# One block for the third attention, the second mixture's routing and its experts

## The reference, cut to what matters

```python
x = x + _L2_xattn_ref(_layernorm(x), ctx, ...)       # 8 heads of 64: softmax(q k / 8) v @ Wo + bo
x = x + _L2_ffn_ref(_layernorm(x), ...)

# _L2_ffn_ref, xf = the normalised tokens (N = 4096)
logits = xf @ Wr + br
topv, topi = top_k(logits, 2)
gates = softmax(topv)
sel = one_hot(topi, 8).sum(1)
rank = cumsum(sel, axis=0) - sel                     # place in the expert's queue, in token order
keep = (sel > 0) & (rank < 1024)                     # capacity
h = gelu(xg @ W1[e] + b1[e]);  out = h @ W2[e] + b2[e]   # xg: the kept tokens of expert e
final[token] += gate * out
```

## Time and profile before

| | us |
|---|---|
| median of three runs (1740.43 to 1750.24) | 1745.27 |
| the profiled execution | 1739.88 |
| its span in the profile | 1738.0 |
| TensorE busy in the span | 1367.1 (79%) |
| DVE busy | 1083.1 (62%) |
| ACT busy | 825.0 (47%) |
| POOL busy | 550.3 (32%) |

### The profile page before, as it was taken

The page is one execution under the profiler, slowest core; times in us unless marked ns, Lnnn a source line. Parts: engine busy times, 40 slices in busy tenths (PEclk is TensorE's granted clock), DMA queues, the critical chain, the costliest instruction groups (busy, mean ns, idle before and its releaser), DMA issues. The chain is left out here.

```text
span 1738.0 us, 43934 instructions
## 1 busy us (share of the span) xinstructions
PE 1367.1 (79%) x14972; PEld 1057.1 (61%) x14972; DVE 1083.1 (62%) x3255; ACT 825.0 (47%) x2117; POOL 550.3 (32%) x990
## 2 busy tenths in 40 slices
PE   6999979986499994149995999994148974678787
PEld 3677655553266674149995888874137763566566
DVE  4888738897899987424443766647401114789764
ACT  1666636665476672412221555541013335677565
POOL 4555411111211105730004644305730007842332
PEclk9999975788699995569997999995569995689798
DMA  4333200000000001137773211101136651111001
GB/s 145 132 112 110 110 27 2 3 3 3 17 23 21 23 17 38 50 112 205 206 205 91 55 40 43 29 12 39 47 110 194 195 150 46 38 24 35 1 13 37
DMA packets 111207, 120.11 MB, mean 69 GB/s; under 512 B 12736, under 2 KB 88512, under 8 KB 110912
## 3 DMA queue, kind: packets, MB, share of 16 engines
q1 hardware_dynamic: 83264, 91.67, 17.5%
q0 software_dynamic: 8192, 16.79, 3.4%
q10 hardware_dynamic: 19584, 9.44, 1.8%
HBM read 81.16 MB, written 36.70 MB: 68 GB/s over the span
## 5 line engine op out<-in xcount | busy, mean ns | idle before, releaser
L2234 PE MATMUL e_H<-e_xT,e_w_up 128*128 128x256 f32 x736 | 173.8, 384 | 0.0
L2080 DVE COPY e_xT<-e_pX 128x256 f32<-128x256 f32 x72 | 30.6, 425 | 216.0 <-PE e_pX L2223 216.0
L2234 PEld LDWEIGHTS e_H<-e_xT,e_w_up 128*128 128x128 f32 x736 | 136.5, 193 | 16.1
L2244 PE MATMUL e_pY<-e_w_down,e_h 128*128 128x128 f32 x992 | 124.4, 277 | 15.8 <-ACT e_h L2156 15.2
L2244 PEld LDWEIGHTS e_pY<-e_w_down,e_h 128*128 128x128 f32 x992 | 119.9, 192 | 27.0 <-issue 19.3
L2145 ACT ACTIVATE e_silu<-e_H 128x256 f32<-128x256 f32 x120 | 42.6, 382 | 162.8 <-DVE e_y L2100 89.7
L2276 POOL DMA_INDIRECT slots_in<-R,r_put x96 | 92.6, 964 | 39.9 <-issue 28.3
L2223 PE MATMUL e_pX<-W,e_rows 128*128 128x128 f32 x144 | 28.6, 282 | 95.1 <-DMA e_rows<-slots_in 93.8
L478 ACT ACTIVATE a_PT<-a_ST 128x1024 f32<-128x1024 f32 x64 | 65.6, 1025 | 77.5 <-PE a_ST L545 77.5
L433 DVE TENSOR_REDUCE a_mx<-a_S 128x8 f32<-128x1024 f32 x64 | 78.1, 1221 | 31.7 <-PE a_S L518 31.5
L2156 ACT ACTIVATE e_h<-e_H,e_w_down 128x256 f32<-128x256 f32 x128 | 50.2, 475 | 85.7 <-DMA e_w_down<-in_f_dram 49.6
(11 more groups left out here) (378 smaller groups left out, 3962.6 us busy)
## 6 DMA issues: line engine op xcount, KB each, us to landing
slots_in<-Y SPq DMA_DIRECT2D x32, 512.0 KB, 3.4
e_w_up<-in_f_dram SPq DMA_DIRECT2D x40, 384.0 KB, 3.1
e_w_down<-in_f_dram SPq DMA_DIRECT2D x32, 322.0 KB, 3.2
e_rows<-slots_in SPq DMA_DIRECT2D x72, 128.0 KB, 2.9
slots_out<-e_y ACTq DMA_DIRECT2D x72, 128.0 KB, 2.9
e_w_up<-in_f_dram SPq DMA_DIRECT2D x32, 256.0 KB, 3.4
e_w_down<-in_f_dram SPq DMA_DIRECT2D x40, 192.0 KB, 2.9
a_cK<-in_ctxT_dram SPq DMA_DIRECT2D x64, 64.0 KB, 1.9
```

Source lines behind the costliest of these rows:

```text
L2234: i = nc.tensor.matmul(H[:, banks * p + b, CHUNK * c:CHUNK * (c + 1)], up[:, p, at:at + P], xT[:, p, :], start=True, stop=True)
L2244: i = nc.tensor.matmul(pY[:, D * s:D * s + D], h[:, p, c, P * s:P * s + P], down[:, p, D * c:D * (c + 1)], start=(c == 0), stop=(c == HC - 1))
```

## The change

`attention2_stage` and the second `mixture_stage` become one block, `attention2_mixture_stage`. Its routing steps follow each tile's residual inside the attention's steps, so the list of each engine grows, and a block now has 48 steps (57 on POOL):

- After a pair's residuals, at lag 11, DVE takes their statistics (`PairNorm`); POOL the root and ACT the norm into `R`, at lag 12.
- TensorE transposes tile v of `R` beside the attention's x transpose (step v + 14); ACT copies both at once; the gate matmul is in step v + 15, in the bank `pV`; DVE takes the logits (`take_l`).
- Six groups (8, 8, 4, 4, 4, 4): the choice in the step of the group's last `take_l`, counts, ranks, places and weights one step later.
- POOL scatters tile v at lag 25 (groups of 8) or 21 (groups of 4).
- The k copy moves from DVE to ACT, the bias add from POOL to DVE.
- The experts' programs follow in the same block; their first weights are loaded behind the attention's last context tile.

```diff
+GROUPS2 = ((0, 8), (8, 16), (16, 20), (20, 24), (24, 28), (28, 32))
...
+        rn = PairNorm(net, sb, sem, "routed")
...                                                     # GpSimd
-            pipeline(pool, NT, [(6, add_bias), (3, lambda u, p: ln.pool_rstd(pool, u, p)),
-                                (0, lambda u, p: combine.gather(u))], straight=True)
+            pipeline(pool, NT, [(3, lambda u, p: ln.pool_rstd(pool, u, p)),
+                                (0, lambda u, p: combine.gather(u)),
+                                (12, when_pair(lambda i, p: rn.pool_rstd(pool, i, p))),
+                                scatter_of(8, 25), scatter_of(4, 21)], straight=True)
...                                                     # VectorE
+            def weigh(g, lo, n):
+                wt, eg = rt.weight[:, :, lo:lo + n], egap[:, g % 2, 0:n]
+                done(dve, s_egap, g)
...
-            pipeline(dve, NT, [(10, normalise), (7, softmax), (5, take_k),
+            pipeline(dve, NT, [(10, normalise), (7, softmax),
                                (1, lambda u, p: ln.vector_moments(dve, u, p)),
                                (2, lambda u, p: ln.vector_apply(dve, u, p)),
+                               (12, when_pair(lambda i, p: rn.vector_shift(dve, i, p))),
                                (0, lambda u, p: combine.add(dve, u)),
-                               (0, lambda u, p: ln.vector_stats(dve, u, p)), (11, residual)], straight=True)
+                               (0, lambda u, p: ln.vector_stats(dve, u, p)), (3, add_bias),
+                               (11, residual), (15, take_l), (16, when_group(ranks)),
+                               (11, when_pair(moments)), (16, when_group(place)), (16, when_group(weigh)),
+                               (15, when_group(choose))], straight=True)
...                                                     # ScalarE, in each step:
+                for lag, fn in ((8, take_pt), (7, exps)):
...
+                if 0 <= t - 3 < NT + 11:
+                    take_xt(t - 3, (t - 3) % 2)
+                for lag, fn in ((10, take_zt), (8, take_v), (4, take_q), (4, take_k), (12, when_pair(apply)),
+                                (16, when_group(exp_gap))):
...                                                     # TensorE
+            def pv_read(t):
+                if t >= 11:
+                    pe.wait_ge(s_x, min(t - 10, NT))
+                if t >= 15:
+                    pe.wait_ge(s_ls, min(t - 14, NT))
+                groups = sum(hi + 15 <= t for lo, hi in GROUPS2)
+                if groups:
+                    pe.wait_ge(s_rank, groups)
...
             def values(u, p):
                 landed(pe, s_cV, u, p)
-                turnsV.take(pe, "v", u)
+                pv_read(u + 8)
...
+            for t in range(NT + 16):
+                if 0 <= t - 8 < NT:
+                    transpose_p(t - 8, t % 2)
+                if t >= 11:
+                    pv_turn(t)
+                for lag, fn in ((16, when_group(counts)), (15, gate), (11, output), (9, product_v),
+                                (10, transpose_z), (8, values), (6, scores)):
...
+                if 0 <= t - 3 < NT + 11:
+                    transposes(t)
+                if 0 <= t - 4 < NT:
+                    project(t - 4, t % 2)
...
-LAYERS = (attention0_stage, feed_forward0, attention1_stage, feed_forward1, attention2_stage, feed_forward2,
+LAYERS = (attention0_stage, feed_forward0, attention1_stage, feed_forward1, attention2_mixture,
           tail_stage)
```

More of the change, by code:

```diff
@@ L1184, in _ @@
+            pipeline(dve, NCH2, [(5, take_e), (1, take_rows)])
         @block.scalar
@@ new lines, in gelu @@
+            def gelu(u, p):
+                landed(act, s_down, u, p)
+                for b in range(BANKS):
+                    act.wait_ge(s_h, BANKS * u + (b + 1))
+                    if b == 0:
+                        free(act, s_e, u)
+                    for c in range(2):
+                        hc = 2 * b + c
+                        i = nc.scalar.activation(h[:, p, hc, :], H[:, BANKS * p + b, CHUNK * c:CHUNK * (c + 1)],
+                                                 ACT.Gelu, bias=down[:, p, HC * D + hc:HC * D + hc + 1])
+                    i.then_inc(s_hs, 1)
@@ new lines, in _, with transpose_rows, hidden @@
+            pe.wait_ge(s_sub, NT)
+            pe.wait_ge(s_zn, NT)
+            pe.wait_ge(s_ks, NT)
+            pe.wait_ge(s_zts, NT)
+            def transpose_rows(u, p):
+                landed(pe, s_r, u, p)
+                free(pe, s_rts, u, bufs=1)
+                for s in range(NSL):
+                    i = nc.tensor.transpose(pX[:, P * s:P * s + P], rows[:, p, s, :], w("ident"))
+                i.then_inc(s_rt, 1)
+            def hidden(u, p):
+                done(pe, s_rts, u)
+                landed(pe, s_up, u, p)
+                free(pe, s_hs, u, per=BANKS)
+                for b in range(BANKS):
+                    for c in range(2):
+                        lo = P * (2 * b + c)
+                        i = nc.tensor.matmul(H[:, BANKS * p + b, CHUNK * c:CHUNK * (c + 1)],
+                                             up[:, p, lo:lo + P], rowsT[:, p, :], start=True, stop=True)
+                    i.then_inc(s_h, 1)
@@ new lines, in expert_output @@
+            def expert_output(u, p):
+                done(pe, s_hs, u, per=BANKS)
+                landed(pe, s_down, u, p)
+                free(pe, s_es, u, bufs=1)
+                for s in range(NSL):
+                    for c in range(HC):
+                        i = nc.tensor.matmul(pY[:, D * s:D * s + D], h[:, p, c, P * s:P * s + P],
+                                             down[:, p, D * c:D * (c + 1)],
+                                             start=(c == 0), stop=(c == HC - 1))
+                i.then_inc(s_e, 1)
@@ L2333, in add, with attention2_mixture @@
         net.nc.vector.tensor_tensor(x, x, rows[1], ALU.add).then_inc(self.s_x, 1)
-def mixture(net, first):
-    rt = Routing(net, first)
-    mixture_stage(net, rt)
+def attention2_mixture(net):
+    rt = Routing(net, first=False)
+    attention2_mixture_stage(net, rt)
     net.routing = rt
@@ L2348, in feed_forward1 @@
 def feed_forward1(net):
[L2349 to L2356 removed]
+    rt = Routing(net, first=True)
+    mixture_stage(net, rt)
+    net.routing = rt
+LAYERS = (attention0_stage, feed_forward0, attention1_stage, feed_forward1, attention2_mixture,
           tail_stage)
```

308 lines of the change are left out of this document (255 added, 53 removed).

## The result

The changed kernel takes 1702.71 us (median of 4 runs, 1700.52 to 1706.87) against 1744.37 us (median of 4, 1740.43 to 1750.24) for the kernel before on the same chip: ratio 0.9761, 95% interval 0.9728 to 0.9795. The forecast was 1705, the range 1684 to 1733: both held.

A forecast was written before the change was run, and what follows sets the result against it. TensorE bounds the attention; 109 us between last residual and experts were to shorten. Terms (a) to (g) put the first expert transpose at 1243.7 instead of 1283.85, 40 us earlier: 1700 us profiled, 1705 median, range 1684 to 1733.

The forecast's parts named there:

- (d): Routing of the two groups of 8 on DVE inside attention steps: 7.2 us a group, 14.4 us together.
- (e): Group 16 to 20 on steps 34 and 35: counts, late normalise in step 36, gates in 36 to 38; 4.6 us.
- (a): One more transpose and gate matmul on TensorE: 0.36 us a step over steps 14 to 34, 7.6 us.
- sign of failure (over 7.5 us): The prediction is wrong if a quiet attention step, forecast at 7.0 to 7.1 us, takes over 7.5 us.
- (b): ACT's k copy and norm applications and DVE's net extra work in attention steps: hidden, 0 us; 4 if the cover fails.
- (c): POOL's norm operations and scatters fit into steps 25 to 31: 0 us, up to 7 if they do not.
- rival 3: POOL falls behind; 24 more scatters after the last indices return 30 us; gain 10, 1735 us; chance 0.08.
- rival 1: DVE's chains are absorbed: (d) shrinks to about 4 us, (e) to 1; gain 54, 1691 us; chance 0.14.
- (f): TensorE's clock falling in waits: 3 us for the waits of (d), 3 us more for the last steps.
- Rival 4: TensorE falls to 1.2 GHz at step 24 and stays there to step 34: 37 slower, 1782 us; chance 0.08.
- (g): From step 39: last residual at 16.1, last indices at 39.4 with clock loss, eight scatters, first expert transpose at 1243.7.
- the forecast's own case: The whole kernel gains 30 to 48 us, 1697 to 1715 us; chance 0.50.

The follow-up runs named there:

- e6: e1 with one repeated set of waits less on TensorE's queue ahead of the gate; 1691.19 us, ratio 0.9712.
- e5: e1 with the k copy back on DVE, behind the softmax of its step; 1694.42 us, ratio 0.9727.
- e2: Changed kernel with places one step later (lag 17) and weights two (lag 18); 1691.51 us, ratio 0.9725.
- e10: e9 with DVE's routing chain spread as in e2 (places at lag 17, weights at 18); 1684.69 us, ratio 0.9673.
- e4: Changed kernel with the scatters of the groups of four at lag 33 instead of 21; 1718.45 us, ratio 0.9857.
- e1: Changed kernel with ACT's exponential of the gaps behind the attention's exponentials instead of last in its step; 1690.88 us, ratio 0.9722.
- e3: Changed kernel without choice, counts, ranks, places, weights and their exponential; rows go to fixed places; 1684.19 us, ratio 0.9678.
- e7: e1 with ACT's copy of the routing's transposed row put behind the z and V copies from step 36 on; 1688.33 us, ratio 0.9707.
- e9: e6 with the transposed row's copy behind the z and V copies in steps 36 to 39 alone; 1688.17 us, ratio 0.9692.
- e8: Edits of e1, e6 and e7 together, scatters one step earlier (lags 24 and 20), against the changed kernel; 1688.15 us, ratio 0.9692.

## Why the prediction was right, and where it was not

It was right in the sum, and in the place of most waits; the sum came out partly by luck, since (d) was 5.8 us too high and (e) 7.4 too low. Up to the start of step 39 it had +29.6 us, measured 33.4 (1194.29 less 1160.92 of the earlier trace rows; 0.4 of it is a later start of the stage and 1.1 comes up to step 14, where no term stood).

(a) The quiet step is 7.24, not 7.05: +0.55 instead of +0.36, 11 us over the steps to 34 instead of 7.6. e6 splits it. With the repeated waits gone 0.38 is left, which is the forecast's own price of one transpose and one gate; 0.17 are waits that were met before. The prediction counted matmuls and not the waits that stand in TensorE's queue ahead of the gate; its own sign of failure (over 7.5 us) was not reached.

(b) Right for the forecast: no quiet step waits for the copy of P, and the move of k to ACT costs nothing there. The value of the move lay where I had not looked. With k on DVE (e5) each of the four steps with a chain of eight tiles is 0.6 us longer; the timed runs don't show it.

(c) and rival 3. Right in the sum: the steps from 25 on stay quiet and in the end eight scatters lie behind the last cast, as forecast. But POOL is late: in step 25 the norm on DVE idles 1.49 us (at 1086.09) behind POOL's two scatters and root, and step 25 stays quiet all the same. With the chain spread (e2, e10) that is no longer hidden and makes up most of the 1.6 us that step 25 is longer. e4 shows that a worse order of the queue costs 9 to 17 us where I had 30.

(d) The place is right: DVE stands at the weights behind ACT's exponential for 2.35 us (forecast 2.4), and product_v starts at 4.5 us into step 24, as forecast (1077.95 less 1073.44). The size is not. Over two quiet steps each, the two groups take 4.8 and 3.8 us, 8.6 where 14.4 were forecast, and 1.1 of it is the clock, which the forecast held apart. What was mis-sized is DVE's backlog ahead of the residual. In step 23 the residual was to come at 4.7 us and hold up the values by 1.6; it came at 3.2, and the step is only 0.5 longer than a quiet one, the price of the counts. In step 24 the values were to wait 2.2 us, until 8.4; they waited 0.19 and started at 7.6 (in step 32, at full clock, they waited 0.53). (The term's own parts, 2.8 and 2.2, make 5.0 and not 5.1.) With the exponential out of the way (e1) the two groups cost 3.3 us, which is rival 1's size for this term.

(e) The step that failed. Steps 35 to 38 take 33.1 us instead of 21.0, +12.0, where (e) had 4.6 (busy time of the four steps, before and then after):

```profile
1139.89:1160.92 21.03, 20.66 (x274) 16.06 (x272) 9.72 (x20) 11.90 (x21) 0.00 (x0) 1.00 0.04 12
```

```profile
1161.24:1194.29 33.05, 26.57 (x290) 20.24 (x289) 17.03 (x68) 15.04 (x33) 12.51 (x16) 0.90 0.15 47
```

It missed ACT's order. The new copy of the routing's row waits for transposes at the end of TensorE's step, and in late steps, with no other work to cover it, it stands in front of the z copy (0.95 us of waiting) and V's (0.57). e3 has it without any chain, and there the four steps are 5.9 us longer than before: 2.85 go with ACT's order (e7), 2.1 are what gate and transpose cost in each quiet step too, 0.9 stay in step 38. The other 6 were the exponential's wait (product_v stands 2.49 us in step 36, where (e) had 3.0) and the half clock behind it, some 3 us that (e) did not have; e1 takes 5.7 back. The prediction looked at what was added on each engine, and had neither the position in ACT's queue nor the clock. The 2.85 us of e7 don't reach the end of the stage, though: the drain takes them back.

(f) The clock. Of the two full groups one fell and one did not. From step 39 to the last residual it ran at 0.74, and e1, at 1.00 there, is 5.3 us faster. In the two full groups 1.1 us were measured where 3 stood; at the end the changed kernel is 5.3 us and e4, of the same order and at 0.91, 2.8 us slower than e1. Without product_v's waits there for the normalise (1.53 and 1.43 us) 3.8 and 1.4 us are left for the clock, so the second 3 was of the right size. The Trainium skill's rule that I set against this change ("TensorE: Matmul & The Clock Gate", section "HAM oscillation — how this bites in real kernels") has each burst behind a wait start cold, in an example whose waits are longer than these; here the first and third group did and the second did not, so the trace agrees in part. Rival 4, which was to price that rule, priced whole steps at the low clock instead, and that is refuted: step 25 takes 7.24.

(g) From step 39: last residual 21.1 us on (forecast 19.1), last cast 42.1 (39.4), then eight scatters and 4.58 us to the first transpose (9.1 and 4.6 forecast). The experts' start is at 1250.3 where 1243.7 was forecast: 3.8 us late at step 39, 2.8 more behind it. The gain in the stage was 33.9 instead of 40, at the lower end of the forecast's own case. The sum was made for a profile, 1700, and the profile took 1706.87; the median is 2.3 us under its point, since the gain of the medians (41.7) is larger than that of the two profiles (33.0). That the point of 1705 was met so closely is partly this scatter.

## What to carry to other kernels

When work moves into the steps of a software pipeline, price its place in each in-order queue, not only its duration. One small operation that stands behind a late producer delays all that follows it, and in the last steps, where nothing covers it, that costs most. Put side work (an exponential for weights needed much later) behind the main chain's operations of the step: here it was worth 14 to 16 us of the stage in the profiles, and 7 us by the two ratios (0.9761 and 0.9722 of 1742), whose intervals overlap. Look at every engine's queue before and after such a move: with the chain spread, DVE waited for a root that stood behind two scatters on POOL. And measure such a fix to the end of the stage: three of them (e7, e9, e10) moved the middle by 2 to 3 us, and the drain, by another wait or by the clock, gave it back.

## What the runs showed of the hardware that was not expected

The same wait does not give the same clock. In the changed kernel product_v waits 2.53 us for DVE in step 24 and again 2.53 us in step 32. Granted clock of both, in windows of 2 us (the column behind POOL's):

```profile
1078.00:1080.00 2.00, 2.00 (x18) 1.66 (x19) 1.91 (x6) 0.63 (x1) 0.00 (x0) 0.54 0.00 0
1080.00:1082.00 2.00, 1.81 (x12) 1.12 (x11) 1.92 (x10) 0.00 (x0) 0.33 (x2) 0.60 0.00 0
...
1140.00:1142.00 2.00, 1.16 (x17) 1.02 (x18) 1.96 (x4) 0.00 (x0) 0.00 (x0) 1.00 0.00 0
1142.00:1144.00 2.00, 1.47 (x12) 0.87 (x12) 1.93 (x12) 0.63 (x1) 0.30 (x2) 1.00 0.00 0
```

```profile
1140.84 1.11 PE L1561 MATMUL a_SO<-a_V,a_PT 128*64 128x130 f32 x16 [2.53 <-DVE a_zn L1260]
```

The 16 matmuls take 1.83 us in the one and 1.11 in the other, and the steps 11.54 and 10.44 us. The matmuls ahead of the wait are the same; what differs is in no row that I have, and it was not tried further. e4 shows it again, with waits of 2.52 and 2.53 us at the same two places: 1.69 us for the 16 matmuls in step 24 and 1.11 in step 32. In e1 a wait of 2.23 us in step 40 left the clock at 1.00 and in e9 one of 2.34 at the same step did not (nor in e7, e8 and e10, 2.34 each). But in e5 one of 2.13 halved it there too, and in the changed kernel one of 2.13 did not. So these runs give no rule for waits of 2.1 to 2.5 us, and an edit that shortens the steps ahead of one (e9) can lose its gain behind it.

Waits that have long been met are not always free on TensorE: 0.17 us a step for a second set of two ahead of the gate, 0.01 for one (e6). And a place in POOL's queue is not a time: e4 puts 32 scatters behind all other work of the queue, and 15 of them have been issued by the last cast.
